# A graph network kernel in two interleaved lanes: products of constants on TensorE in the first and the last half

## The chip, the cores and the metric

The kernel runs on one NeuronCore of a Trainium2 chip. The time is the device time of one execution in microseconds (us). Engine names are those of the profile: PE is TensorE's matmul, PEld its weight load, DVE is VectorE, ACT is ScalarE, POOL is GpSimd, SP is SyncE, which issues the transfers. "PEclk" is the TensorE clock that was granted, as a share of 2.4 GHz; it takes two levels in this trace, 1.0 (2.4 GHz) and 0.5 (1.2 GHz), so a share between them says how a stretch is mixed.

## What is computed

Sixteen graphs of 512 nodes with 128 features pass through eight layers, each on a layer norm of x and each added back to x:

```python
x = x + _L0_gnn_ref(_layernorm(x), adj, ...)   # three GRU steps over messages A^T (h W)
x = x + _L0_ffn_ref(_layernorm(x), ...)        # 8 experts, top 2 of a router
x = x + _L1_gnn_ref(_layernorm(x), adj, ...)   # graph attention, softmax over neighbours
x = x + _L1_ffn_ref(_layernorm(x), ...)        # slice attention, 8 heads
x = x + _L2_gnn_ref(_layernorm(x), adj, ...)   # mean over neighbours
x = x + _L2_ffn_ref(_layernorm(x), ...)        # a state space block in chunks of 128
x = x + _L3_gnn_ref(_layernorm(x), adj, ...)   # masked attention, 2 layers x 4 heads x 4 row tiles
x = x + _L3_ffn_ref(_layernorm(x), ...)        # routed MLP, top half of the tokens
```

Nothing crosses from one graph to another. x is 16 x 512 x 128 in float32, adj 16 x 512 x 512 in int32.

## The kernel before

One graph is four tiles of 128 rows (T = 4). Its state stays in SBUF from the first layer to the last: X, the normalised XN, its transpose XT, the adjacency in float32 (AF) and as a mask (NM), and a scratch area. There are two sets of these buffers, the two lanes; graph g uses lane g mod 2.

The eight layers are cut in an early phase (g0, f0, g1, f1) and a late phase (g2, f2, g3, f3). `halves` runs them as a software pipeline of 17 steps: in step h the early phase of graph h and the late phase of graph h-1 run together. So the step h = 0 has an early phase alone (graph 0), the step h = 16 has a late phase alone (graph 15), and the 15 steps between have both. These two outer steps are the "first half" and the "last half" of this text; in them one lane is alone.

Each engine's program is written by its own generators. A generator yields at each place where its engine would wait; a step between two yields is one turn: first the wait on a semaphore, then the instructions behind it. In a shared step a string of letters per engine (PE_TURNS, DVE_TURNS, ...) says whose turn is next, "e" for early and "l" for late. In the first and the last half the strings were not used: the generator simply ran out. The order of each engine is thus fixed when the program is written; when an instruction starts is decided by semaphores.

PSUM has eight banks: the early phase uses banks 0 to 2 (`ep`), the late phase banks 3 to 7 (`lp`, where lp(4) is bank 7). In the first half banks 3 to 7 are free, in the last half banks 0 to 2.

All matmuls are written through the helper at L457 and transposes by `pe.transpose`. A float32 matmul stands in the trace as two passes, a transpose and a bfloat16 matmul as one. The instructions named below: L466 are the four transposes of XN behind every layer norm (`to_columns`), L482 and L519 those of the GRU state, L900 the four transposes of one head's probabilities in the masked attention (`g3_turn`, one turn for each of 16 heads and row tiles and each of 2 layers), L632 and L652 those of the slice attention. On DVE L1328, L1331 and L1334 are helpers (tensor_tensor, tensor_scalar, scalar_tensor_tensor), L1814 is the masked maximum and L1831 a copy from PSUM; ACT has one helper, L1045; POOL L1973 is the root of the layer norm.

Two constants of the preparation matter: `ident_bf`, the 128x128 identity in bfloat16, and `bias_parts`, 128 x 512 in bfloat16, of which three rows hold the parts of a bias and the others are zero. Both are complete before the block with the halves starts.

Of the kernel before, what the change touches and what calls it, by code (L numbers as in the profile page):

```python
# [24 lines left out]
P = 128  # L25
# [50 lines left out]

SP_TURNS = (
    "leleel"
)
PE_TURNS = (  # L80
    "leeeeellllelllllleeeeeellllllllelleeeeelelelleellllleeeeeeeeeellllllllelllleeeeellllelllleleeeelelee"
# [41 lines left out]
def build(nc, x, adj, weights, raw, out):  # L123
    graphs = x.shape[0]
# [9 lines left out]
    with ctx:  # L134
        def sb(name, shape, dt=F32):
            return ctx.enter_context(nc.sbuf_tensor(name, shape, dt))
# [6 lines left out]
        ident_bf = sb("ident_bf", [P, P], BF16)  # L143
        ones_bf = sb("ones_bf", [P, P], BF16)
        bias_parts = sb("bias_parts", [P, SH * SG], BF16)
# [36 lines left out]
        def ep(i, n=512, rows=P, at=0):  # L182
            return EP[i][0:rows, at:at + n]

        def lp(i, n=512, rows=P, at=0):
            return LP[i][0:rows, at:at + n]
# [221 lines left out]
        def phase(stages, g):  # L408

            for stage in stages:  # L410
                yield from stage(g)

        def halves(turns, early, late):

            for h in range(graphs + 1):
                first = phase(early, h) if h < graphs else iter(())
                second = phase(late, h - 1) if h else iter(())
                for turn in turns if 0 < h < graphs else "":
                    next(first if turn == "e" else second, None)
                for _ in first:  # L420
                    pass
                for _ in second:
                    pass

        with nc.Block() as block:

            @block.sync
            def _(sp):
                def loads(g):
                    yield  # L430
                    if g + LANES < graphs:
                        sp.wait_ge(*done("x_new", g, 0))
                        sp.dma_start(XIN[g][:, :, :], x_rows[g + LANES]).then_inc(s[f"x_loaded{g % LANES}"], 16)
                    yield
                    if g + LANES < graphs:
                        sp.wait_ge(*done("adjf_ready", g))
                        sp.dma_start(ADJ[g][:, :, :], adj_rows[g + LANES]).then_inc(s[f"adj_loaded{g % LANES}"], 16)

                def stores(g):
                    c_rows = SC[g][MS:P, F2_XS + 2 * N:F2_XS + 3 * N]  # L440
                    yield
                    sp.wait_ge(*done("silu_ready", g))
                    sp.dma_start(cut(g, F2_CC, N, MS), c_rows).then_inc(s[f"cc_ready{g % LANES}"], 16)
                    sp.dma_start(SC[g][MS:P, F2_CC:F2_CC + N], c_rows).then_inc(s[f"cc_ready{g % LANES}"], 16)
                    yield
                    sp.wait_ge(*done("x_new", g, 7))
                    sp.dma_start(out_rows[g], X[g][:, :, :]).then_inc(s[f"stored{g % LANES}"], 16)

                halves(SP_TURNS, (loads,), (stores,))
                for b in lanes:  # L450
                    sp.wait_ge(*landed("stored", graphs - LANES + b))
# [3 lines left out]
            def _(pe):  # L455
                def mm(o, lhsT, rhs, start=True, stop=True, **k):
                    return pe.matmul(o, lhsT, rhs, start=start, stop=stop, **k)  # L457
# [573 lines left out]
                def f3(g):  # L1031
# [4 lines left out]
                            yield from f3_rank(g)  # L1036
                    yield from f3_out(g)

                halves(PE_TURNS, (g0, f0, g1, f1), (g2, f2, g3, f3))


            @block.scalar
            def _(act):
# [271 lines left out]
                def f3(g):  # L1315
                    yield from columns_out(g, F3)
                    for k in range(FH // P):
                        yield from f3_hidden(g, k)

                halves(ACT_TURNS, (g0, f0, g1, f1), (g2, f2, g3, f3))  # L1320


# [814 lines left out]
```

## Time and profile before

| | |
|---|---|
| median of 3 runs | 3650.3 us (3647.51 to 3654.89) |
| profiled execution, its own time | 3651.31 us |
| its span, first to last instruction | 3649.3 us |
| PE busy | 3051.0 us, 84% |
| DVE busy | 2288.5 us, 63% |
| ACT busy | 1894.7 us, 52% |
| POOL busy | 776.8 us, 21% |
| granted TensorE clock, mean | 0.948 |
| chain that ended last | PE 60%, DVE 19%, ACT 12%, issue 5%, POOL 2% |

The profiled execution is 1.0 us above the median, and 2.0 us of its time lie outside the span. The chain that ended last is followed back from the last instruction: at each step to what released it, or to the instruction before it on its engine. A "busy" PE includes the time in which a result still travels through the array.

### The profile page before, as it was taken

How to read it: one execution, taken by the hardware profiler on the slowest of the kernel's cores; microseconds unless marked ns; L12 is line 12 of the kernel's file. 1: busy time of each engine (PE TensorE's matmuls, PEld its weight loads, DVE VectorE, ACT ScalarE, POOL GpSimd, SP SyncE). 2: the span in 40 equal slices, each digit the busy share in tenths (PEclk: the TensorE clock that was granted, in tenths of full speed). 3: DMA queues.
4: the chain of work that ended last, by engine and by line, in shares of the span. 5: the costliest groups of instructions: out<-in, count | busy, mean ns of one | idle time of the engine just before them, and what ended most of it. 6: DMA issues, size and time to landing. Idle time of an engine off the chain costs nothing.

```text
span 3649.3 us, 50559 instructions
## 1 busy us (share of the span) xinstructions
PE 3051.0 (84%) x18590; PEld 2003.9 (55%) x18622; DVE 2288.5 (63%) x7012; ACT 1894.7 (52%) x3318; POOL 776.8 (21%) x836
## 2 busy tenths in 40 slices
PE   5688888888888888888888888888988888898856
PEld 2455555555555555555555555555555555555533
DVE  3356675757667675666757566675756767566642
ACT  1235565474545646464464646546454654755433
POOL 0012222122222212222121122212112221212211
PEclk8889999999999999999999999999999999999977
DMA  2000000000000000000000000000000000000000
GB/s 109 15 4 15 4 18 1 21 1 7 15 4 18 1 9 13 7 15 2 20 1 7 15 4 18 1 21 1 7 15 4 18 1 7 1 7 1 4 3 4
DMA packets 28438, 39.91 MB, mean 11 GB/s; under 512 B 1312, under 2 KB 17696, under 8 KB 27936
## 3 DMA queue, kind: packets, MB, share of 16 engines
q1 hardware_dynamic: 28192, 36.67, 3.1%
q8 instruction: 149, 2.44, 0.3%
q14 instruction: 97, 0.79, 0.1%
HBM read 28.28 MB, written 4.19 MB: 9 GB/s over the span
## 4 chain that ended last, share of the span: by engine, by line
PE 60%; DVE 19%; ACT 12%; issue 5%; POOL 2%; DVEq 0%; ACTq 0%; POOLq 0%
PE ps L457 47%; ACT scratch L1045 7%; PE ps L900 6%; DVE scratch L1328 6%; DVE scratch L1334 3%; PE ps L466 3%; DVE scratch L1814 2%; ACT L1045 2%; ACT adjf L1045 2%; POOL rstd L1973 2%; DVE scratch L1331 1%; DVE stats L1349 1%; DVE x L1334 1%; PE ps L632 1%; ACT xT L1045 1%
## 5 line engine op out<-in xcount | busy, mean ns | idle before, releaser
L457 PE MATMUL ps<-scratch 128*128 128x128 f32 (+6 forms) x4608 | 566.9, 394 | 130.1 <-DVE scratch L1328 53.6
L1045 ACT ACTIVATE scratch<-scratch 128x512 f32<-128x512 f32 (+4 forms) x768 | 528.0, 690 | 217.8 <-DVE scratch L1328 91.8
L457 PE MATMUL ps<-xT,weights_sb 128*128 128x512 f32 x1152 | 575.6, 612 | 34.2 <-ACT xT L1045 22.0
L2010 POOL TENSOR_SCALAR scratch<-scratch 128x512 f32<-128x512 f32 x512 | 362.4, 723 | 937.5 <-DVE scratch L1821 936.9
L457 PEld LDWEIGHTS ps<-scratch 128*128 128x128 f32 (+5 forms) x4608 | 356.4, 165 | 261.0 <-issue 94.0
L457 PE MATMUL ps<-weights_sb,scratch 128*128 128x128 f32 (+2 forms) x3456 | 480.5, 280 | 2.1 <-DVE scratch L1472 1.4
L457 PEld LDWEIGHTS ps<-weights_sb,scratch 128*128 128x128 f32 (+2 forms) x3456 | 431.1, 190 | 80.5 <-issue 46.8
L1045 ACT ACTIVATE scratch<-ps 128x512 f32<-128x512 f32 (+2 forms) x512 | 286.1, 568 | 299.1 <-PE ps L457 164.1
L900 PE MATMUL ps<-weights_sb,scratch 128*128 128x128 f32 x2048 | 332.9, 287 | 114.0 <-ACT adjf L1045 64.4
L1973 POOL TENSOR_TENSOR rstd<-ve,minus_half 128x4 f32<-128x4 f32 x126 | 142.4, 1130 | 1202.5 <-DVE ve L1331 1202.5
L1045 ACT ACT_TABLE_LOAD x292 | 374.6, 1283 | 5.0
L900 PEld LDWEIGHTS ps<-weights_sb,scratch 128*128 128x128 f32 x2048 | 236.5, 146 | 254.8 <-issue 178.6
L1814 DVE CUSTOM_DVE_ANT_0 scratch<-ps,nomask 128x512 f32<-128x512 f32 x512 | 335.1, 683 | 43.0 <-PE ps L457 43.0
L1045 ACT ACTIVATE scratch<-ps,weights_sb 128x512 f32<-128x512 f32 x416 | 276.3, 687 | 118.2 <-PE ps L457 116.5
L1045 ACT ACTIVATE xT<-ps 128x512 f32<-128x512 f32 x112 | 66.9, 597 | 510.0 <-PE ps L466 510.0
L457 PEld LDWEIGHTS ps<-xT,weights_sb 128*128 128x128 f32 x1152 | 199.5, 194 | 199.0 <-issue 134.1
L1334 DVE SCALAR_TENSOR_TENSOR x<-ps,scratch,x 128x128 f32<-128x128 f32 x576 | 162.1, 344 | 197.5 <-PE ps L457 177.3
L1328 DVE TENSOR_TENSOR scratch<-scratch 128x512 f32<-128x512 f32 (+6 forms) x304 | 237.5, 794 | 29.7 <-ACT scratch L1045 24.6
L457 PE MATMUL ps<-adjf,scratch 128*32 128x256 f32 (+1 forms) x1280 | 244.9, 431 | 0.0
L1045 ACT ACTIVATE adjf<-ps 128x512 f32<-128x512 f32 x320 | 187.9, 592 | 105.7 <-PE ps L900 100.8
L1045 ACT ACTIVATE scratch<-ps,made_sb 128x512 f32<-128x512 f32 x128 | 87.9, 687 | 237.8 <-PE ps L457 237.7
L457 PE MATMUL ps<-weights_sb,xT 128*128 128x128 f32 x1152 | 186.6, 288 | 26.8 <-ACT xT L1045 26.3
(166 smaller groups left out, 4263.1 us busy)
## 6 DMA issues: line engine op xcount, KB each, us to landing
adj<-adj SPq DMA_DIRECT2D x16, 1024.0 KB, 5.5
weights_sb<-weights SPq DMA_DIRECT2D x1, 5104.0 KB, 22.0
x_in<-x SPq DMA_DIRECT2D x16, 256.0 KB, 2.9
scratch<-scratch SPq DMA_DIRECT2D x32, 128.0 KB, 2.3
out<-x SPq DMA_DIRECT2D x16, 256.0 KB, 2.3
scratch<-raw SPq DMA_DIRECT2D x1, 2029.0 KB, 10.5
```

Of the source, the lines that this page charges most:

```text
L457: return pe.matmul(o, lhsT, rhs, start=start, stop=stop, **k)
L466: last = pe.transpose((ep if k < G2 else lp)(0, P, P, t * P), rows[:, t, 0:D], ident)
L632: last = pe.transpose(ep(2, P, P, k * P), cut(g, F1_SW + t * N, N)[:, tile(k)], ident)
L900: last = pe.transpose(lp(4, P, P, j * P), probabilities(g, layer, n)[:, tile(j)], ident)
L1045: return act.activation(o, a, func, **k)
L1328: return v.tensor_tensor(o, a, c, op)
L1331: return v.tensor_scalar(o, a, s1, s2, op0, op1, **k)
L1334: return v.scalar_tensor_tensor(out=o, in0=a, scalar=s1, in1=c, op0=op0, op1=op1, **k)
L1349: last = v.bn_stats(stats[g][:, t, :], src[:, t, 0:D])
L1814: v.tensor_tensor_reduce(probabilities(g, layer, n), lp(n % AH), NM[g][:, n // AH, :], -1.0, 4 * BIG, ALU.add, ALU.min, cut(g, G3_MX + n, ...
L1973: pool.tensor_tensor(rstd[g][:, :], ve[g][:, :], minus_half[:, :], ALU.pow).then_inc(s[f"rstd_ready{g % LANES}"], 1)
L2010: pool.tensor_scalar(p, p, cut(g, G3_RI + n, 1), 1.0, ALU.mult, ALU.mult).then_inc(s["att_p"], 1)
```

## The change

In the first and the last half, before a turn of PE's generator is taken, PE gets a number of products of the two constants, each 128 x 256 in bfloat16, started and stopped by itself. Nothing reads what they write: in the first half bank 7, in the last bank 0. They wait for nothing and nothing waits for them. How many stand ahead of which turn is a digit in base 36 in two strings, at most 35 ("z"). FIRST_PAUSES has 401 products at 28 places, LAST_PAUSES 573 at 52. The shared steps get none. On DVE, ACT, POOL and SP the instructions and their order stay as they were.

```diff
+FIRST_PAUSES = (
+    "006000000000x000000000x000000000xy00080000000000000000000000000000000000000000000b0000z0006070802b96"
+    "000z00064j05m70000o760c66"
+)
+LAST_PAUSES = (
+    "00000600000z000600060z00214000z0000003p000z0006000ds09c0078c00600048c7787760001000ds09c0078c00600048"
+    "c7787760003000z00060007"
+)
...
-        def halves(turns, early, late):
+        def halves(turns, early, late, keep=None):
 
             for h in range(graphs + 1):
                 first = phase(early, h) if h < graphs else iter(())
                 second = phase(late, h - 1) if h else iter(())
-                for turn in turns if 0 < h < graphs else "":
-                    next(first if turn == "e" else second, None)
+                if 0 < h < graphs:
+                    for turn in turns:
+                        next(first if turn == "e" else second, None)
+                elif keep:
+                    alone, pauses = keep[h > 0], (FIRST_PAUSES, LAST_PAUSES)[h > 0]
+                    for n in pauses:
+                        alone(int(n, 36))
+                        next(second if h else first, None)
                 for _ in first:
                     pass
                 for _ in second:
                     pass
...
-                halves(PE_TURNS, (g0, f0, g1, f1), (g2, f2, g3, f3))
+                def keep_first(n):
+                    for _ in range(n):
+                        mm(lp(4, 2 * P), ident_bf[:, :], bias_parts[:, 0:2 * P])
+
+                def keep_last(n):
+                    for _ in range(n):
+                        mm(ep(0, 2 * P), ident_bf[:, :], bias_parts[:, 0:2 * P])
+
+                halves(PE_TURNS, (g0, f0, g1, f1), (g2, f2, g3, f3), (keep_first, keep_last))
```

The lines of the changed file are shifted by 14, so L457 is L471 there, L466 L480, L482 L496 and L900 L914.

Three places on PE. The first is the end of a GRU step in the first half, where PE has written the three gates and waits for the new state (`h_ready`). Before:

```order
L457 MATMUL ps2<-scratch0,made_sb 128x512 [waits aggr_ready]
L457 MATMUL ps1<-scratch0,made_sb 128x512
L457 MATMUL ps0<-scratch0,made_sb 128x512
L482 MATMUL ps1<-weights_sb,xT0 128x128 [waits h_ready]
L482 MATMUL ps1<-weights_sb,xT0 128x128 x3
```

After:

```order
L471 MATMUL ps2<-scratch0,made_sb 128x512 [waits aggr_ready]
L471 MATMUL ps1<-scratch0,made_sb 128x512
L471 MATMUL ps0<-scratch0,made_sb 128x512
L471 MATMUL ps7<-bias_parts,ident_bf 128x256 x33
L496 MATMUL ps1<-weights_sb,xT0 128x128 [waits h_ready]
L496 MATMUL ps1<-weights_sb,xT0 128x128 x3
```

The 33 products stand between the last gate and the wait; nothing else has moved.

The second is the layer norm behind the neighbour mean in the last half, where PE waits for the normalised rows (`xn_ready1`) and then for their transpose in SBUF (`xT_ready1`). Before:

```order
L457 MATMUL ps6<-xn1,adjf1 128x129 x8
L466 MATMUL ps3<-weights_sb,xn1 128x128 [waits xn_ready1] x4
L457 MATMUL ps6<-xT1,weights_sb 128x512 [waits xT_ready1]
L457 MATMUL ps4<-xT1,weights_sb 128x512
L457 MATMUL ps5<-xT1,weights_sb 128x512
```

After:

```order
L471 MATMUL ps6<-xn1,adjf1 128x129 x8
L471 MATMUL ps0<-bias_parts,ident_bf 128x256 x35
L480 MATMUL ps3<-weights_sb,xn1 128x128 [waits xn_ready1] x4
L471 MATMUL ps0<-bias_parts,ident_bf 128x256 x6
L471 MATMUL ps6<-xT1,weights_sb 128x512 [waits xT_ready1]
L471 MATMUL ps4<-xT1,weights_sb 128x512
L471 MATMUL ps5<-xT1,weights_sb 128x512
```

Both waits have products ahead of them now, the long one as many as a digit allows.

The third is in the masked attention of the last half: one turn is four transposes of a head's probabilities into bank 7, which a copy on DVE (`pT_dve`) or ACT (`pT_act`) must empty before the next turn. Before:

```order
L900 MATMUL ps7<-weights_sb,scratch1 128x128 [waits att_p]
L900 MATMUL ps7<-weights_sb,scratch1 128x128 x3
L900 MATMUL ps7<-weights_sb,scratch1 128x128 [waits pT_dve,att_p]
L900 MATMUL ps7<-weights_sb,scratch1 128x128 x3
L900 MATMUL ps7<-weights_sb,scratch1 128x128 [waits pT_act,att_p]
```

After:

```order
L914 MATMUL ps7<-weights_sb,scratch1 128x128 [waits att_p]
L914 MATMUL ps7<-weights_sb,scratch1 128x128 x3
L471 MATMUL ps0<-bias_parts,ident_bf 128x256 x9
L914 MATMUL ps7<-weights_sb,scratch1 128x128 [waits pT_dve,att_p]
L914 MATMUL ps7<-weights_sb,scratch1 128x128 x3
L471 MATMUL ps0<-bias_parts,ident_bf 128x256 x12
L914 MATMUL ps7<-weights_sb,scratch1 128x128 [waits pT_act,att_p]
```

Between two turns now stand 7 to 12 products, which write bank 0 and not the bank of the transposes.

## Rows read from the trace of the kernel before

**Rows 1.** Busy time by stretch: start:end, length, engines (instructions), PEclk, DMA share, GB/s.

```profile
50.00:228.00 178.00, 126.23 (x518) 79.77 (x521) 66.41 (x183) 43.06 (x69) 11.32 (x10) 0.78 0.02 8
228.00:3453.00 3225.00, 2787.33 (x17372) 1835.09 (x17400) 2131.77 (x6519) 1786.56 (x3120) 729.78 (x778) 0.97 0.03 9
3453.00:3649.30 196.30, 120.79 (x640) 77.53 (x640) 75.80 (x255) 63.57 (x127) 33.54 (x42) 0.73 0.01 3
```

**Rows 2.** Chain of waits by line, in the first half and in the last.

```profile
by line: PE ps L457 60.9%; ACT scratch L1045 5.2%; DVE scratch L1328 3.9%; PE ps L466 2.7%; DVE scratch L1331 2.3%; issue 2.2%; POOL rstd L1973 1.7%; DVE x L1334 1.7%; DVE stats L1349 1.5%; ACT xT L1045 1.5%; PE ps L632 1.4%; POOL scratch L
...
by line: PE ps L457 38.4%; PE ps L900 13.4%; ACT scratch L1045 6.4%; issue 6.2%; ACT adjf L1045 4.9%; DVE scratch L1814 4.2%; DVE scratch L1334 3.9%; DVE scratch L1328 3.6%; DVE scratch L1331 3.0%; PE ps L466 2.5%; POOL rstd L1973 2.1%; DVE
```

**Rows 3.** The stretches at 1.2 GHz in both halves, each view with its sum.

```profile
50.00:60.30 10.30, 6.50 (x11) 3.04 (x12) 3.93 (x7) 2.57 (x3) 0.00 (x0) 0.50 0.00 0
...
176.30:183.10 6.80, 4.12 (x7) 2.05 (x9) 1.89 (x7) 0.60 (x1) 2.27 (x2) 0.50 0.00 0
...
sum 78.50, PE 58.51 PEld 39.76 DVE 22.62 ACT 12.87 POOL 4.46; mean PE 6.50 PEld 4.42 DVE 2.51 ACT 1.43 POOL 0.50
...
3456.50:3459.90 3.40, 2.84 (x13) 2.84 (x14) 0.00 (x0) 1.10 (x2) 0.00 (x0) 0.50 0.00 0
3466.80:3477.00 10.20, 6.28 (x10) 2.92 (x11) 2.74 (x15) 2.95 (x5) 2.10 (x2) 0.50 0.00 1
...
3497.50:3504.30 6.80, 5.14 (x34) 4.92 (x36) 5.86 (x15) 0.61 (x1) 0.64 (x1) 0.50 0.00 0
3518.00:3524.80 6.80, 5.33 (x11) 2.75 (x12) 1.12 (x4) 0.60 (x1) 0.35 (x1) 0.50 0.00 0
...
sum 107.30, PE 78.29 PEld 47.53 DVE 29.54 ACT 40.18 POOL 24.79; mean PE 6.02 PEld 3.66 DVE 2.27 ACT 3.09 POOL 1.91
```

**Rows 4.** Pieces of the chain of waits in the attention's second layer: start, us, what.

```profile
3601.35 1.97 PE ps L457 x32
3603.87 0.64 PE ps L900 x4
...
3609.17 1.10 PE ps L900 x4
...
3618.60 3.68 PE ps L457 x32
```

**Rows 5.** Timeline, passes in a row at either clock: start, us, engine, instruction, count.

```profile
63.73 2.84 PE L457 MATMUL ps<-scratch,made_sb 128*128 128x512 f32 x6
...
3471.97 3.78 PE L457 MATMUL ps<-xT,weights_sb 128*128 128x512 f32 x4 [0.69 <-ACT xT L1045]
...
3448.76 2.73 PE L457 MATMUL ps<-scratch 128*128 128x128 f32 x23
3448.87 2.42 PEld L457 LDWEIGHTS ps<-scratch 128*128 128x128 f32 x21
...
3457.06 3.40 PE L457 MATMUL ps<-weights_sb,xT 128*128 128x128 f32 x16 [0.69 <-ACT xT L1045]
```

**Rows 6.** Loads of bfloat16 with bias_parts (ns: least, median, most), and such a product's timeline.

```profile
L457 PEld LDWEIGHTS ps<-bias_parts,ones_bf x64: 97/98/151, 181.0 to 3416.9; 128*128 128x128 bf16 x64
...
3413.04 0.38 PE L457 MATMUL ps<-bias_parts,ones_bf 128*128 128x512 bf16 x1
3413.26 0.60 PE L900 MATMUL ps<-weights_sb,scratch 128*128 128x128 f32 x4
```

**Rows 7.** Timeline, PE behind waits of both halves; in brackets PE's idle time before.

```profile
70.14 0.83 PE L482 MATMUL ps<-weights_sb,xT 128*128 128x128 f32 x4 [3.57 <-DVE xT L1328]
...
178.08 1.24 PE L466 MATMUL ps<-weights_sb,xn 128*128 128x128 f32 x4 [6.77 <-DVE xn L1331]
...
3470.04 1.25 PE L466 MATMUL ps<-weights_sb,xn 128*128 128x128 f32 x4 [6.00 <-DVE xn L1331]
...
3499.16 1.22 PE L457 MATMUL ps<-scratch 128*128 128x128 f32 x4 [5.42 <-DVE scratch L1328]
...
3557.61 1.09 PE L900 MATMUL ps<-weights_sb,scratch 128*128 128x128 f32 x4 [0.78 <-ACT scratch L1045]
```

## Prediction

> **What bounds the kernel now.** I read the busy times by stretch first. In the 3225 us in which two lanes run together PE is busy for 2787 us at a mean clock of 0.97; in the first half it is busy for 126.2 of 178.0 us at 0.78, in the last for 120.8 of 196.3 us at 0.73 [rows 1]. The reader is to see that the change touches 374.3 us of the span and that both halves have what it speaks of: PE idle for 51.8 and 75.5 us, together 127.3 us, and a clock that is often low. The chain of waits comes next, because a slow clock costs only where PE is the one that is waited for. In three of its groups alone PE holds 65.0% of the chain in the first half (115.7 us) and 54.3% in the last (106.6 us) [rows 2]. That is 222.3 of PE's 247.0 busy us, or 0.90: with one lane there is no other work to hide PE's.
>
> Last I put the stretches at 1.2 GHz side by side. They make 78.5 us in the first half with 58.5 us of PE work, and 107.3 us in the last with 78.3 us of PE work [rows 3]. So 136.8 us of PE work run at the low level, and by the share of 0.90 some 123 us of them lie on the path that sets the end.
>
> **What the low clock costs.** The same work stands in the trace at both levels. Four transposes of the attention take 1.10 us on the chain at 1.2 GHz and 0.64 at 2.4, its 32 value products 3.68 and 1.97 us [rows 4]; passes of 512 columns take 3.78 us for four and 2.84 us for six, 0.945 and 0.473 us each [rows 5]. The saving is 42%, 46% and 50%; the time in which a result leaves the array does not halve. I take 46%. If all of the 123 us ran at 2.4 GHz, the end would come 56.6 us sooner.
>
> **What the products cost.** There are 974 of them, each a load and one pass over 256 columns in bfloat16. None stands in the trace. The nearest row is a bfloat16 pass of 512 columns at 2.4 GHz: the next instruction starts 0.22 us behind it, half the 0.473 us of a float32 pass of that width [rows 5, 6]. A product then takes about 0.109 us at 2.4 GHz, and twice that, 0.213 us, at 1.2 GHz, where a float32 pass of 128 columns, which needs as many clock periods, is 3.40 us for 16 [rows 5]. Does the load stay hidden? In the row of 23 such passes at 2.4 GHz the loads run alongside and the pair takes 2.73/23 = 0.119 us, with the tail of the last in it, though each pass has its own load [rows 5]. A bfloat16 load is 97 ns [rows 6], shorter than the pass that it has to hide under. I take it as hidden, so the 974 products are 106 us of PE's time. From below the bound is 0.109, from above the sum of load and pass, 0.206 us.
>
> Put against the waits: 33 products are 3.60 us, in a wait of 3.57 us behind a GRU step; 7 are 0.76 us, in a wait of 0.78 us of the attention [rows 7]. The counts fit at 2.4 GHz. At 1.2 GHz the 33 would be 7.0 us and the 7 would be 1.5 us, so every wait would end late. Products that overhang delay real work: the instruction behind them on PE is the one that the chain comes back to. A few places get 3 or 4 products though PE hardly waits there, or one or two more than fit; for all of these at 2.4 GHz I take 2 us, between nothing and the 12 us that one extra product at each of the 80 places and a third of a microsecond at ten would give. They write banks that nobody uses, wait for nothing, and the order on the other four engines is the same, so there is no other price.
>
> **Where the clock will not hold.** A digit ends at 35 products, 3.8 us. Four waits are longer, from 5.42 to 6.77 us; three of them stand in the rows, 6.77, 6.00 and 5.42 us [rows 7], so 1.6 to 3.0 us stay empty. Behind each of the four the clock is low now, for 4.12, 6.28, 5.14 and 5.33 us of PE work [rows 3]. If it fell again at all four, 46% of that, 9.6 us, would not be saved, and the six products that follow at three of the places would overhang by 3 x 6 x 0.104 = 1.9 us: 11.5 us in all. I take half, 5.7 us, since shorter empty stretches do not always make it fall. The first 6.50 us of PE work of the first half and the 2.84 us behind the first layer norm of the last half have no long run of products ahead, and I leave them at 1.2 GHz: 9.3 x 46% = 4.3 us.
>
> **Where something else is next in line.** When a turn of the attention shrinks by 0.46 us, the copy that empties the bank, the exponentials on ACT or the maxima on DVE can be the next to be late. For all of the 32 turns that would be 14.7 us. In most of the rows of the chain a turn is PE, one copy, PE, so I take 3 us.
>
> **Sum.** 56.6 - 4.3 - 5.7 - 2 - 3 = 41.6 us. The profiled execution took 3651.3 us in its own time, so 3609.7; the median of the runs stands 1.0 lower, so I forecast 3609 us.
>
> **Rivals.**
>
> *The load isn't hidden.* Then a product is 0.206 us even at 2.4 GHz, and 974 of them are 200.6 us in waits of 127.3: 73 us overhang. Against the 43.6 us that the rest of the sum gains that makes the kernel 30 us slower, 3680 us. It decides from about 0.176 us for a product, (127.3 + 43.6)/974. For it speaks that no row shows two bfloat16 products in a row; against it the 23 passes at 0.119 us with as many loads. The Trainium skill (TensorE: Matmul & The Clock Gate, Part 3, The mechanism) says that a weight load overlaps a running matmul only when it goes to another row group, and all of these go to the same one. With its figures for a load (107 ns) and a pass (109 ns) the products would be 210 us and the kernel some 40 us slower. The rows of 23 contradict it, and by them I give this 0.04.
>
> *The products don't count as work for the clock.* Most of their moving rows are zeros and the standing operand is an identity. Then the clock stays as it is, nothing is gained, and products are at 0.213 us where it is low. Of the 450 products in runs of up to 13, 254 stand behind work that is at 1.2 GHz now: 254 x 0.104 = 26 us slower, 3677 us. Nothing in the trace shows what such data do; 0.07.
>
> *The clock holds only in part.* It falls behind all four long waits and also in the attention, where products and transposes alternate; each fall makes products overhang before it rises again. I put it at 8 to 30 us gained, with 3631 us in the middle: 41.6 less the other half of the falls (5.7) and less half of what the 32 turns are to give (7.4), with some 8 us of overhang. For it speaks that after a fall the clock now stays low for 6.8 and 10.2 us [rows 3]; against it that with products in the waits PE is hardly idle there. 0.15.
>
> *Nothing happens*, because PE's time is only turned into a wait for others. Against it stands the chain's share of 0.90. 0.04, 3650 us.
>
> **How the numbers follow.** The forecast's case has 0.70. Its own range is 3598 to 3620 us: without any fall and with nothing next in line 41.6 + 5.7 + 3 = 50.3 us are gained, with all falls and 8 us next in line 31. The range of 3597 to 3633 us adds the part held case. A measurement of this kernel can tell about 0.2%, 7.3 us, from no change. Faster by more: 0.70 and nearly all of the 0.15, 0.85. Within it: 0.04. Slower: 0.04 + 0.07 = 0.11.
>
> **What the profile will show.** The mean clock of the first half should rise from 0.78 to above 0.93 and that of the last from 0.73 to above 0.88, with low stretches left at about 53 to 60 us, near 3457, and behind some of the four long waits. Rows of products should start 0.11 us apart at 2.4 GHz. The GRU wait should be filled, with the four transposes behind it starting within 0.1 us of DVE's end. The turns of the attention should take 1.4 to 1.5 us each where one now takes 1.10 and a wait of 0.78 us [rows 4, 7]. The first half should be 18 to 22 us shorter, the last 20 to 25, the middle the same within 2 us. The prediction is wrong if products start 0.2 us apart, if PEclk in the halves stays below 0.8, or if the clock is at 1 and PE's waits grow by what its work shrinks.

## The result, and the profile after

The changed kernel takes 3603.2 us (median of 4, 3601.7 to 3606.5) beside 3650.5 us of the kernel before; the ratio is 0.9869 with a 95% interval from 0.9857 to 0.9881. The profiled execution has 3604.15 us in its own time, 47.2 less than that of before. The forecast was 3609 us in a range from 3597 to 3633.

The busy times by stretch of the changed kernel, cut where PE's last real work of the first half ends and where the last half begins (start:end, length, PE, PEld, DVE, ACT, POOL, PEclk, DMA share, GB/s):

```profile
50.00:204.50 154.50, 146.70 (x923) 102.06 (x924) 65.97 (x182) 42.93 (x69) 11.32 (x10) 0.97 0.03 9
204.50:3429.10 3224.60, 2786.31 (x17400) 1829.97 (x17398) 2131.65 (x6519) 1785.76 (x3120) 728.00 (x778) 0.97 0.03 9
3429.10:3602.10 173.00, 156.83 (x1213) 117.11 (x1213) 75.55 (x255) 63.32 (x127) 33.47 (x42) 0.94 0.02 4
```

Against [rows 1] the first half is 23.5 us shorter, the last 23.3, and the middle, cut at the same work, has not moved (3224.6 us for 3225.0). The clock rose from 0.78 to 0.97 and from 0.73 to 0.94. PE's busy time rose although the halves shrank; that is the products.

The GRU wait, in the timeline of the changed kernel (start, us, engine, instruction, count; in brackets the idle time before, absent where there is none):

```profile
61.98 2.84 PE L471 MATMUL ps<-scratch,made_sb 128*128 128x512 f32 x6
64.66 3.77 PE L471 MATMUL ps<-bias_parts,ident_bf 128*128 128x256 bf16 x33
68.39 0.66 PE L496 MATMUL ps<-weights_sb,xT 128*128 128x128 f32 x4
```

The 33 products take 3.77 us, of which 0.27 us are the record of the last one, so they start (3.77 - 0.27)/32 = 0.109 us apart. The distance from the six gate passes to the transposes, 6.41 us, is that of before, to 0.01 us [rows 5, 7]: the wait is full and nothing overhangs. The transposes behind it take 0.66 us, where they took 0.83 before; four of them take 0.64 us at 2.4 GHz and 1.10 at 1.2 [rows 4].

Turns of the attention on the chain of waits of the changed kernel, in the stretch that was at 1.2 GHz before:

```profile
3568.99 0.63 PE ps L914 x4
3569.61 0.76 PE ps L471 x7
3570.39 0.63 PE ps L914 x4
3571.02 0.87 PE ps L471 x8
...
3576.11 1.97 PE ps L471 x32
```

The transposes are at 0.63 us each and the 32 value products at 1.97, the high level of [rows 4]. A turn with 7 products takes 1.40 us, where it was 1.10 and a wait of 0.78 [rows 4, 7]; one with 8 takes 1.51. The reader must not be misled by the chain: it names the products as what PE did last, but they end with the copy that PE waits for; the wait has only become busy.

What is left at 1.2 GHz from the first transposes on, as stretches of the changed kernel with the same columns as above:

```profile
53.40:56.80 3.40, 3.40 (x12) 1.96 (x11) 0.64 (x1) 0.60 (x1) 0.00 (x0) 0.50 0.00 0
166.00:169.50 3.50, 3.50 (x9) 1.55 (x7) 0.47 (x1) 0.44 (x1) 0.77 (x1) 0.51 0.00 0
3432.40:3435.90 3.50, 3.50 (x20) 3.26 (x18) 0.00 (x0) 1.19 (x2) 0.00 (x0) 0.53 0.00 0
3446.20:3449.70 3.50, 3.50 (x12) 2.26 (x13) 0.63 (x4) 0.60 (x1) 1.09 (x1) 0.51 0.00 0
3463.30:3470.10 6.80, 6.58 (x30) 6.08 (x31) 4.61 (x13) 1.93 (x5) 0.74 (x1) 0.50 0.01 2
3494.00:3497.50 3.50, 3.50 (x12) 1.96 (x12) 0.15 (x1) 0.60 (x1) 0.00 (x0) 0.51 0.00 0
```

And what PE does at two of them, in the timeline:

```profile
164.71 1.10 PE L480 MATMUL ps<-weights_sb,xn 128*128 128x128 f32 x4 [2.95 <-DVE xn L1353]
...
3446.10 1.25 PE L480 MATMUL ps<-weights_sb,xn 128*128 128x128 f32 x4 [2.17 <-DVE xn L1353]
3447.14 1.49 PE L471 MATMUL ps<-bias_parts,ident_bf 128*128 128x256 bf16 x6
3448.42 1.06 PE L471 MATMUL ps<-xT,weights_sb 128*128 128x512 f32 x1
```

The waits that 35 products cannot fill stay open for 2.95 and 2.17 us, and the clock falls behind them. At the second, the six products then run at 1.2 GHz, take 1.49 us and hold up the 512-column pass: it starts 2.32 us behind the transposes, where it was 1.93 before [rows 5, 7]. The clock does not fall there every time. In another profiled execution of the same kernel (e9 below) both waits are as long, the stretches behind them are at 2.4 GHz, and the six products take 0.82 us:

```profile
165.61 1.10 PE L480 MATMUL ps<-weights_sb,xn 128*128 128x128 f32 x4 [2.95 <-DVE xn L1353]
166.55 0.82 PE L471 MATMUL ps<-bias_parts,ident_bf 128*128 128x256 bf16 x6
...
3450.00:3453.50 3.50, 3.47 (x13) 1.82 (x14) 0.00 (x0) 1.99 (x4) 1.04 (x1) 1.00 0.00 0
```

### The profile page after: what moved, and what is told of

Its sections match the earlier page's. It is cut to its first block, busy times and chain, and to the rows that moved or that the text cites. A ratio compares the mean times of both kernels' runs of the same rounds, so it can differ in the third digit from the quotient of the medians.

```text
span 3602.1 us, 52539 instructions
## 1 busy us (share of the span) xinstructions
PE 3106.5 (86%) x19596; PEld 2060.7 (57%) x19596; DVE 2287.9 (64%) x7012; ACT 1893.5 (53%) x3318; POOL 775.0 (22%) x836
## 4 chain that ended last, share of the span: by engine, by line
PE 62%; DVE 18%; ACT 11%; issue 5%; POOL 2%; DVEq 0%; ACTq 0%; POOLq 0%
PE ps L471 49%; PE ps L914 6%; ACT scratch L1067 6%; DVE scratch L1350 5%; PE ps L480 3%; DVE scratch L1356 3%; ACT L1067 2%; DVE scratch L1836 2%; ACT adjf L1067 2%; POOL rstd L1995 2%; DVE stats L1371 1%; DVE scratch L1353 1%; DVE x L1356 1%; PE ps L646 1%; DVE xn L1353 1%
## 5 line engine op out<-in xcount | busy, mean ns | idle before, releaser
L471 PE MATMUL ps<-scratch 128*128 128x128 f32 (+6 forms) x4608 | 550.2, 385 | 116.8 <-DVE scratch L1350 45.6
L471 PE MATMUL ps<-xT,weights_sb 128*128 128x512 f32 x1152 | 566.1, 603 | 32.5 <-ACT xT L1067 20.6
L471 PEld LDWEIGHTS ps<-scratch 128*128 128x128 f32 (+5 forms) x4608 | 344.7, 161 | 244.5 <-issue 89.8
L471 PE MATMUL ps<-weights_sb,scratch 128*128 128x128 f32 (+2 forms) x3456 | 478.1, 279 | 0.2 <-DVE scratch L1494 0.2
L471 PEld LDWEIGHTS ps<-weights_sb,scratch 128*128 128x128 f32 (+2 forms) x3456 | 428.3, 189 | 78.1 <-issue 47.0
L914 PE MATMUL ps<-weights_sb,scratch 128*128 128x128 f32 x2048 | 322.0, 280 | 91.0 <-ACT adjf L1067 53.1
L914 PEld LDWEIGHTS ps<-weights_sb,scratch 128*128 128x128 f32 x2048 | 230.0, 143 | 225.3 <-issue 153.5
L471 PEld LDWEIGHTS ps<-xT,weights_sb 128*128 128x128 f32 x1152 | 196.8, 192 | 193.3 <-issue 130.7
L471 PE MATMUL ps<-adjf,scratch 128*32 128x256 f32 (+1 forms) x1280 | 241.4, 425 | 0.0
L471 PE MATMUL ps<-weights_sb,xT 128*128 128x128 f32 x1152 | 183.0, 284 | 23.4 <-ACT xT L1067 23.3
```

Of the source, the lines that this page charges most:

```text
L914: last = pe.transpose(lp(4, P, P, j * P), probabilities(g, layer, n)[:, tile(j)], ident)
```

## The experiments

Each kernel is built from the changed one and compared with the kernel before on its own chip. The theory is that the gain is the clock, kept high because PE's array streams during waits, in each half by itself. The rivals are that a queue which never runs dry is what helps; that only long idle stretches matter; that data with work in them is needed.

**One half each.**

```diff
-                halves(PE_TURNS, ..., (keep_first, keep_last))
+                halves(PE_TURNS, ..., (keep_first, lambda n: None))      # e1
+                halves(PE_TURNS, ..., (lambda n: None, keep_last))       # e2
```

> The products of the last half are left out, the 401 of the first half stay. Theory (each half gains by its own clock, nothing else is touched): the first half is 154 us as in the changed kernel, the last 196 us as before, so 24 us faster than before, 3626 us. Rival (the gain has a shared part, as a clock or an instruction stream that stays better for the whole run): clearly more than 24 us, or the middle shorter than 3224 us.

> The products of the first half are left out, the 573 of the last half stay. Theory: the last half is 173 us, the first 178 us, 23 us faster than before, 3627 us. Rival (shared part): the two kernels with one half each would not add up to the 47 us of both.

e1: 3630.2 us beside 3649.1, ratio 0.9949 [0.9934, 0.9964], 19 us. e2: 3624.9 us, ratio 0.9935 [0.9921, 0.9950], 24 us. The stretches show more than the sums. Of e1:

```profile
50.00:204.50 154.50, 146.51 (x923) 102.03 (x924) 66.11 (x183) 42.95 (x69) 11.33 (x10) 0.97 0.03 9
204.50:3432.30 3227.80, 2789.32 (x17401) 1829.14 (x17398) 2130.46 (x6519) 1787.46 (x3120) 729.24 (x778) 0.97 0.03 9
3432.30:3628.70 196.40, 120.86 (x640) 77.55 (x640) 75.81 (x255) 63.57 (x127) 33.50 (x42) 0.73 0.01 3
```

Of e2:

```profile
50.00:225.90 175.90, 122.57 (x522) 78.02 (x523) 68.59 (x186) 43.13 (x69) 11.32 (x10) 0.83 0.02 8
225.90:3450.10 3224.20, 2787.76 (x17401) 1830.71 (x17399) 2130.40 (x6519) 1787.17 (x3120) 729.38 (x778) 0.97 0.03 9
3450.10:3623.50 173.40, 157.16 (x1213) 117.27 (x1213) 75.63 (x255) 63.34 (x127) 33.54 (x42) 0.94 0.02 4
```

A half without products stays at a low clock, one with them is as in the changed kernel. The two gains, 19 and 24, make 43 of the 47 us. e2 came out as expected; e1 is 4 us slower than expected, with an interval of its gain from 13 to 24 us. Two things differ between executions that no product touches. The middle takes 3224.2 us in e2 and 3227.8 in e1. And in e2 the clock is at 2.4 GHz in the first stretch already, where it was at 1.2 before [rows 3]:

```profile
50.00:60.30 10.30, 4.13 (x8) 2.21 (x9) 6.22 (x10) 1.51 (x3) 0.00 (x0) 1.00 0.00 0
```

From PE's first transposes for the first graph to those for the second it is 174.9 us before (53.11 to 228.02), 170.3 in e2 (55.48 to 225.78) and 151.5 in the changed kernel (52.81 to 204.31). Beside the first half of e2 the products of the first half bring 18.8 us and not 23, which is what e1 measured. No shared part is needed.

**Narrow products.**

```diff
-                        mm(lp(4, 2 * P), ident_bf[:, :], bias_parts[:, 0:2 * P])
+                        mm(lp(4, 8), ident_bf[:, :], bias_parts[:, 0:8])
```

> The same 974 products at the same places, but 8 columns wide in place of 256. Theory (the gain is the clock, and the clock follows the array's work): the array has next to nothing more to do, the clock of both halves stays near 0.78 and 0.73 and the time within 8 us of before, 3643 to 3652 us. Rival (instructions on the queue are what helps, as a real matmul starts sooner behind a stream than behind a wait, or the weight loads count as work): nearly the whole 47 us, 3603 to 3615 us.

3647.8 us beside 3649.1, ratio 0.9995 [0.9985, 1.0004]: nothing. In the GRU wait of this kernel the 33 loads and products are issued and PE is idle all the same; the last half as a stretch stays as it was before:

```profile
68.17 0.97 PE L471 MATMUL ps<-bias_parts,ident_bf 128*128 128x8 bf16 x33
71.90 1.11 PE L496 MATMUL ps<-weights_sb,xT 128*128 128x128 f32 x4 [2.76 <-DVE xT L1350]
...
3450.20:3646.70 196.50, 135.42 (x1213) 100.27 (x1213) 75.72 (x255) 63.57 (x127) 33.51 (x42) 0.73 0.01 4
```

33 narrow products are over in 0.97 us, so this removes the array's work and with it the filling of the wait. What it excludes is that 974 more instructions and loads by themselves bring anything. That a queue which never runs dry helps in itself is answered by the GRU wait of the changed kernel: behind its full wait the transposes start no sooner, 6.41 us after the first gate pass as before. The first half of e3, 176.0 us at 0.83, is that of e2.

**Zeros.**

```diff
+                v.memset(still_bf[:, :], 0.0)
+                v.memset(moving_bf[:, :], 0.0)
...
-                        mm(lp(4, 2 * P), ident_bf[:, :], bias_parts[:, 0:2 * P])
+                        mm(lp(4, 2 * P), still_bf[:, :], moving_bf[:, :])
```

> The same products at the same places, but both operands are tiles of zeros. Theory (the clock follows whether the array streams, not what): the same as the changed kernel, 3603 us within 4, clock 0.97 and 0.94 in the halves. Rival (data that change something count more; the identity with three live rows was only just enough): the clock falls back and the time rises to 3640 us or more, with overhangs.

3606.7 us beside 3646.7, ratio 0.9888 [0.9871, 0.9904]. The halves are as in the changed kernel:

```profile
50.00:204.60 154.60, 146.20 (x923) 101.92 (x924) 66.53 (x183) 42.93 (x69) 11.31 (x10) 0.97 0.03 9
...
3431.90:3605.00 173.10, 156.79 (x1213) 117.13 (x1213) 75.64 (x256) 63.31 (x127) 33.48 (x42) 0.94 0.02 4
```

Zeros keep the clock of these halves as the constants do. The rival "the products don't count as work" is out in its strongest form.

**Half of the products, the long runs alone, the short runs alone.**

```diff
-                        alone(int(n, 36))
+                        alone(int(n, 36) // 2)                            # e4
+                        alone(int(n, 36) if int(n, 36) > 13 else 0)       # e5
+                        alone(int(n, 36) if int(n, 36) <= 13 else 0)      # e6
```

> Half of the products at each place (rounded down), 445 or so. Theory (the array has to be busy for most of a stretch to have the high clock): a wait half filled keeps the clock in some places and loses it in others; 20 to 40 us of the 47 stay, clock of the halves between 0.85 and 0.93. Rival (a few products are enough, since it is the long idle stretch alone that makes the clock fall): all 47 us and perhaps 3 more, since overhangs vanish, 3600 to 3604 us.

> Only the 17 runs of more than 13 products stay (524 products), the 63 short ones (450) are left out. Theory (the clock falls behind long waits in the first half, but in the attention of the last half it stays low because the many short waits of 0.8 us leave the array too idle to rise again): the first half keeps nearly all of its 24 us, the last half gains 6 to 12 of its 23; 3615 to 3622 us. Rival (only long idle stretches matter): both halves keep all, 3603 us or less.

> Only the 63 runs of up to 13 products stay (450), the long ones (524) are left out. Theory: the clock falls at every long wait and the short runs then stand at 1.2 GHz, where each overhangs, but they help it to rise again in the attention; 5 to 20 us gained, nearly all in the last half, 3630 to 3645 us. Rival (products at 1.2 GHz cost more than they bring): slower than before, above 3658 us.

| | us | beside | ratio | first half, clock | last half, clock |
|---|---|---|---|---|---|
| e4, half | 3607.5 | 3649.1 | 0.9890 [0.9875, 0.9905] | 158.2, 0.92 | 173.2, 0.92 |
| e5, long | 3634.3 | 3646.7 | 0.9963 [0.9948, 0.9977] | 161.4, 0.92 | 191.8, 0.80 |
| e6, short | 3629.6 | 3646.7 | 0.9949 [0.9934, 0.9964] | 164.2, 0.87 | 178.9, 0.87 |

e4 has 468 products, not the 445 that I wrote. The stretches are those of one execution each: in e5 and e6 the middle takes 3229.5 and 3229.3 us, 4.9 and 4.7 more than in the changed kernel with the same instructions, and the profiled execution of e6 is the fastest of its four (3624.5 to 3632.3 us). By their medians the whole kernels gain 12 us (e5) and 17 (e6).

My expectations held for e4 at its upper edge of gain, missed e5 by 12 us and held e6 just about (3629.6 for 3630 to 3645). Half of the products keep the whole gain of the last half (173.2 against 173.0 us) and lose 4 us of the first. So the theory behind my expectation was too strict. The long runs alone give the last half only 4.5 of its 23 us: between the turns of the attention there is no long wait, and its clock stays low without the short runs. I had thought that the first half would keep nearly all with the long runs; it keeps 17 of 24. The short runs alone are worth 14 of the first half's 24 us and 17 of the last's 23.

**Longer runs at the open waits.**

```diff
+FIRST_LONGER = {86: 38, 94: 16, 103: 61}
+LAST_LONGER = {0: 34, 11: 55, 24: 14, 30: 48, 37: 0, 42: 51, 51: 25, 83: 25, 114: 41}
...
-                    for n in pauses:
-                        alone(int(n, 36))
+                    longer = (FIRST_LONGER, LAST_LONGER)[h > 0]
+                    for k, n in enumerate(pauses):
+                        alone(longer.get(k, int(n, 36)))
```

> The changed kernel with other counts at ten places: waits that 35 products leave open get as many as fill them (38, 61, 55, 48, 51, 41), the first layer norm of the last half gets 34 where it had none, the wait ahead of the state space block's running sum 14 for 2 and one attention softmax 16 for 8; three places whose products overhang get fewer (0 for 3, 25 for 28 twice). Theory (what is left at 1.2 GHz comes from these open waits, and the overhangs from the products at them): the clock is at 1.0 in both halves from 57 us on, and another 5 to 9 us go, 3594 to 3598 us. Rival (these stretches are off the path or the clock falls for another reason): 3603 us.

3597.3 us beside 3646.7, ratio 0.9861 [0.9846, 0.9876], and 3595.6 to 3597.6 in all four executions.

```profile
50.00:200.60 150.60, 149.63 (x960) 105.12 (x961) 63.49 (x177) 42.92 (x69) 11.32 (x10) 0.99 0.03 10
...
3426.40:3593.60 167.20, 158.65 (x1291) 118.83 (x1288) 75.42 (x255) 63.02 (x127) 33.51 (x42) 1.00 0.02 4
```

The last half has the full clock throughout and takes 5.8 us less than in the changed kernel. The first stretch is cut at 50 us, where this execution started 3 us earlier; from PE's first transposes to its last work it takes 150.6 us against 151.7. So 5.8 and 1.1, together 6.9 us, come from the places whose counts were changed, in these two executions. In the whole kernel the size is less certain. The medians stand 9.4 us below e7, which has the counts of the changed kernel, on the same chip; e11 beside e9 below gives 4.0; and the ratios of e8 and of the changed kernel, 0.9861 and 0.9869, have intervals that overlap. That there is a gain is clear: no execution of e8 takes more than 3597.6 us, and none of the changed kernel, here or in e9, less than 3601.6.

**The same in the shared steps.** In each of the 15 shared steps the clock falls where PE waits for the last GRU state.

```diff
                 def g0_back(g):
                     yield
+                    if g:
+                        pe.wait_ge(*done("r_ready", g, GNN0_STEPS - 1))
+                        for _ in range(24):
+                            mm(ep(2, 2 * P), ident_bf[:, :], bias_parts[:, 0:2 * P])
                     pe.wait_ge(*done("h_ready", g, GNN0_STEPS - 1))
```

> The changed kernel itself once more, to stand on the same chip beside the two that follow. Theory: 47 us faster than before, ratio 0.987.

> The changed kernel, and in each of the 15 shared steps 24 products ahead of PE's last wait for the GRU state, into the bank of the reset gate behind a wait until that gate is read. In the trace of the changed kernel PE idles there for 2.95 us and the clock falls for 6.8 us in each shared step. Theory (an idle wait costs the same in a shared step as in a half alone, with about 5.8 us of PE work at 1.2 GHz behind it): 15 times 1.5 to 2.7 us less, 3565 to 3582 us. Rival (with two lanes the other engines are next in line, or the second lane's sparse work lets the clock fall anyway): 3598 to 3606 us; slower if the products hold up the late lane's turns on PE.

> The kernel with longer runs and the products of the shared steps together. Theory: the two gains add up, 6 us and whatever the products of the shared steps give by themselves. Rival: the phase in which the clock falls decides and they don't add up within 5 us.

e9: 3603.1 us beside 3650.5, ratio 0.9865 [0.9849, 0.9882]. e10: 3607.5, ratio 0.9878 [0.9863, 0.9893]. e11: 3599.1, ratio 0.9857 [0.9842, 0.9871]. I had expected 3565 to 3582 us of e10 and missed it by 25 us: the products of the shared steps bring nothing. e10 is 4 us above the control, which is within the intervals. The longer runs bring their part also beside them (e11 is 8 us below e10). One shared step, in e9:

```profile
1123.72 0.71 PE L471 MATMUL ps<-scratch 128*128 128x128 f32 x4 [0.38 <-DVE scratch L1356]
1127.38 1.11 PE L533 MATMUL ps<-weights_sb,xT 128*128 128x128 f32 x4 [2.95 <-DVE xT L1350]
1128.51 2.99 PE L471 MATMUL ps<-made_sb,scratch 128*128 128x128 f32 x16
...
1133.13 0.60 PE L480 MATMUL ps<-weights_sb,xn 128*128 128x128 f32 x4
```

The same in e10:

```profile
1124.88 0.77 PE L471 MATMUL ps<-scratch 128*128 128x128 f32 x4 [0.89 <-DVE scratch L1360]
1125.44 4.44 PE L471 MATMUL ps<-bias_parts,ident_bf 128*128 128x256 bf16 x24
1129.71 0.60 PE L537 MATMUL ps<-weights_sb,xT 128*128 128x128 f32 x4
1130.15 1.95 PE L471 MATMUL ps<-made_sb,scratch 128*128 128x128 f32 x16
...
1134.16 1.10 PE L480 MATMUL ps<-weights_sb,xn 128*128 128x128 f32 x4 [0.27 <-DVE xn L1357]
```

The 24 products take 4.44 us in a wait of 2.95: the clock falls just as they start, and rises again while they run. The stretches of e10:

```profile
1125.40:1128.70 3.30, 3.30 (x18) 2.34 (x17) 3.09 (x6) 0.00 (x0) 0.00 (x0) 0.50 0.02 5
...
1133.50:1136.00 2.50, 1.49 (x8) 0.74 (x6) 1.19 (x5) 0.70 (x1) 1.20 (x2) 1.00 1.00 355
```

So the 16 passes behind take 1.95 us where they took 2.99, and the transposes 0.60 for 1.11. But from the passes on the last state to the transposes of the GRU it is 4.83 us where it was 3.66, an overhang of 1.2 us. And from there to the layer norm's transposes it is 4.45 us instead of 5.75, so the whole way is 9.28 us against 9.41 (1124.88 to 1134.16 and 1123.72 to 1133.13). There PE waits for DVE: the layer norm's transposes are at 2.4 GHz and still take 1.10 us for 0.60, because DVE writes the four parts of xn from 1133.76 to 1134.88 us. In the control PE came last, and DVE had xn ready at 1133.05. The chain of waits says the same, first in e9, then in e10:

```profile
1128.51 4.79 PE ps L471 x32
...
1130.35 0.70 DVE x L1354
...
1132.70 1.03 POOL rstd L1999
...
1133.76 0.20 DVE xn L1357
```

In e9 it goes over PE's 32 passes, in e10 over the layer norm on DVE and POOL, which no clock of PE shortens. Over all 15 shared steps the mean clock rises from 0.97 to 0.98, and the middle takes 3227.6 us where the control takes 3228.5. Of the two rivals, that the other engines are next in line is the one that the step shows. It was looked at in one step; how much the overhang takes in the others was not measured.

## Why the prediction was right

The mechanism, the direction and the size were right: 41.6 us forecast, 47.2 measured. By its steps:

- **What the low clock costs.** Right. Four transposes went from 1.10 to 0.63 us, the 32 value products from 3.68 to 1.97, as [rows 4] had them.
- **What the products cost.** Right. They start 0.109 us apart, at the lower bound. The load is hidden; the rival with 0.206 us is out. The Trainium skill's rule (TensorE: Matmul & The Clock Gate, Part 3, The mechanism) that a load overlaps only with another row group does not hold here: 33 loads to the same one went under 33 products.
- **Where the clock will not hold.** The four long waits cost me 5.7 us and the first layer norm of the last half 1.3, together 7.0; filling them and the few places around them gave 6.9 us in the profiled execution (e8). That the two agree so closely is in part luck. The clock fell behind three of the four and not behind that of 5.42 us, but in its place at 3463 us, ahead of which 2 products left a wait of 1.35 us open; and in e9, the same kernel, it fell behind one of the four and at 3465 us.
- **What is next in line.** This is a term that was mis-sized: I took off 3 us. The turns with 7 and 8 products gave 0.45 to 0.47 us each where they had been at 1.2 GHz. The turns with 12 gave none: one takes 1.94 us at 1.2 GHz before (3543.10 to 3545.04), and 1.93 in the changed kernel (3565.65 to 3567.58), since DVE's maxima and ACT's exponentials come last there. Three of the six such turns stood at 1.2 GHz before, so the price of the turns is 1.4 us.
- **The first stretch.** I left 6.50 us of PE work at 1.2 GHz, a price of 3.0 us. In the changed kernel the clock rose at 56.8 us and not at 60.3. What of it the six products did stays open: in e5, which leaves them out, it rose at about 60 us, but in e2, without them too, it was high from 50 us on.
- **The share on the chain.** 0.90 came from three groups of rows and left the smaller ones of PE out; the other 10% would be worth up to 6 us. Together with the two terms above, this is more than the 5.6 us by which I fell short; how they split, and what overhangs took, was not measured.
- **Rivals.** That the products don't count was given 0.07: zeros hold the clock as well (e7). That nothing happens was given 0.04: narrow products show what that looks like (e3). That the clock holds only in part, at 0.15, is what happened when the long runs or the short ones were left out (e5, e6), not with all of them.
- **The numbers beside the time.** The last half and the middle came out as I said; the first half became 23.5 us shorter in the profiled execution, for 18 to 22. The range of the forecast's own case was rounded outwards: 3650.3 less 50.3 and 31 us is 3600 and 3619, not 3598 and 3620.

The best kernel of the study is e8.

## What to carry to other kernels

Where PE stands on the chain and its clock is low, look at the same instructions at both levels: the difference times the low stretches on the chain is what products in the waits can bring, here 47 of 374 us. Size each run to its wait at the high clock (wait divided by 0.109 us for 256 columns); half of that kept most of the gain here (e4). Fill the longest waits completely, since products that start at the low clock overhang, and do not leave out the short waits of a stretch that consists of them. Before adding a run, look at the clock at its start and at which engine would come last behind it: in the shared steps here the clock fell as the products started, and behind them the layer norm on DVE and POOL was next in line, so a higher clock bought no time.

A stretch read from one execution can be off by some us though its instructions are the same: the middle took from 3224.2 to 3229.5 us, and a first half without wide products 174.9 or 170.3 us. A gain of that size needs the medians of several executions beside it.

## What the runs showed of the hardware

Products of zeros keep the clock as well as any: 0.97 and 0.94 in the halves (e7). 974 products of 8 columns with their loads don't: the last half stays at 0.73 (e3). With half of the products both halves have 0.92 (e4). The clock does not fall behind the same wait every time: with 2.95 and 2.17 us left open it fell in the one profiled execution of the changed kernel and not in the other (e9). Sixteen transposes are work for the clock too. In the timeline of the kernel before they start at 3490.33 us, and nothing else is on PE until 3499:

```profile
3490.33 3.41 PE L795 MATMUL ps<-weights_sb,scratch 128*128 128x128 f32 x16 [0.57 <-DVE scratch L1721]
```

They run at 1.2 GHz to their end, and the clock of the stretch behind them, in which PE is idle, is at 2.4, in its stretches:

```profile
3490.70:3494.10 3.40, 3.04 (x15) 2.64 (x13) 2.43 (x10) 2.11 (x4) 0.74 (x1) 0.51 0.00 0
3494.10:3497.50 3.40, 0.00 (x0) 0.00 (x0) 1.98 (x8) 1.67 (x3) 2.97 (x2) 1.00 0.00 0
```
